# A cross-attention slot reordered: GpSimd's row sums wait for VectorE's next subtraction

## The chip, the cores and the metric

The kernel runs on one core of one Trainium2 chip. The metric is the device time of one execution in microseconds (us). Three runs of the kernel before gave 1718.86, 1724.16 and 1724.18 us; their median is 1724.16 us.

## What is computed

One perceiver layer in fp32: cross attention of 8 batches of 128 queries on 2048 context rows each (width 512, 16 heads of 32), then a causal differential self attention, then a dense mixture of 8 experts. The change touches the cross attention only. Cut to what matters:

```python
q = (layernorm(x) @ wq.T + bq)          # 8 x 128 x 512, heads of 32
k = (ctx @ wk.T + bk)                   # 8 x 2048 x 512
v = (ctx @ wv.T + bv)
scores = einsum('bhqd,bhkd->bhqk', q, k) / sqrt(32)
attn = softmax(scores, axis=-1)
o = einsum('bhqk,bhkd->bhqd', attn, v)  # then x = x + o @ wo.T + bo
...
x = x + differential_attention(layernorm(x)); x = x + experts(layernorm(x))
```

## The kernel before

The cross attention (`cross_attention`) works through 32 score slots (8 batches x 4 head groups; a head group is 4 heads, `HG`). A slot `m` has four chunks `c` = 0 to 3 of 512 context rows, so there are 128 chunks `n = 4m + c`. Beside the scores the same loop projects the keys and values of later context: piece `p` of 512 context rows, in four key products (`keys`) and four value products (`values`), each of 12 matmuls (the fp32 numbers are split into a high and a low half, and `product`, lines 41 to 45, multiplies high with high, high with low and low with high).

Every engine walks the same loop over beats, and a slot is eight beats. In its own walk an engine does, for each beat, what the small functions of lines 475 to 511 name, in the order in which the code asks for them. This order, together with semaphores, is all that sets the order of the work. The text below calls a beat by its remainder r0 to r7 modulo 8.

What a slot does:

- TensorE (lines 757 to 782): at the even beats scores of one chunk into `psS` (`column_scores`, L709: c2 at r0, c3 at r2, c0 at r4, c1 at r6); at every beat one product (r0 to r3 keys, r4 to r7 values); at r2 and r6 the weighted values of two chunks (`outputs`, L723) ahead of the scores; at r0 the denominators (`denominators`, L746), first thing in the beat; at r3 it turns the running maxima (L754, "M"), at r4 the spread maxima back (L754, "B"), after the product of the beat.
- ScalarE (lines 787 to 862): evicts the product of the beat before (L798 keys, L810 and L819 values); at r5 copies the maxima rows (`mb`, L826); at even beats rounds a quarter of the turned context to its high half (L835), at r4 writes `spread` (L838), at even beats takes the exponentials of a chunk (L843), at r0 adds the value bias to the outputs (L850); at odd beats moves a chunk of scores from `psS` to SBUF (L860), which frees `psS` for TensorE.
- VectorE (lines 875 to 923), at even beats: at r4 the maxima per row (`top`, L881); the subtraction of the maxima from a chunk of scores (L888); at r0 reciprocal and division of the outputs (L903, L907); the low half of the context quarter (L911); a transpose of the next quarter (L871); then four maxima over the new scores (L920, L923).
- GpSimd (lines 636 to 651): sums the exponentials of a chunk into `acc`: one addition for c0 (L645, which also waits for the denominators of the slot before), two for the others (L650). It starts when the exponentials of the chunk are done (L640).

The subtraction and the exponentials of chunk n stand ten beats behind its scores: exponentials of c0 at r6, c1 at r0, c2 at r2, c3 at r4. A context quarter has the number k = 0 at r0, 1 at r2, 2 at r4, 3 at r6. The sums of chunk n free a buffer for the move of chunk n + 7 (L859). The outputs of a slot's first chunk wait for the division of the slot before (`od_free`, L718). The last four slots (`TAIL` = 28 on) have no GpSimd sums; TensorE sums their chunks itself (L737), inside `outputs`. No projections are left there from beat 256 on.

Of the kernel before, what the change touches and what calls it, by code (L numbers as in the profile page):

```python
# [47 lines left out]
def f32(ap):  # L48

    return ap.bitcast(F32)  # L50
# [398 lines left out]
def cross_attention(nc, x, ctx_in, w, q_d, o_d, cin, kT, shared):  # L449

    with ExitStack() as ctx:
# [18 lines left out]
        def steps(beat, first, every, count):  # L470

            n, r = divmod(beat - first, every)
            return n if r == 0 and 0 <= n < count else None

        def transposed(beat):

            n = steps(beat, -SLOT, 2, SLOTS * CHUNK)
            return None if n is None or n < 2 * CHUNK else divmod(n, CHUNK)
# [14 lines left out]
        def turned_slot(beat):  # L493
            return steps(beat, 27, SLOT, SLOTS)
# [2 lines left out]
            return steps(beat, 28, SLOT, SLOTS)  # L497

        def exp_step(beat):
            return steps(beat, 30, 2, SLOTS * CHUNK)  # L500

        def value_steps(beat):

# [3 lines left out]
        def sum_slot(beat):  # L507
            return steps(beat, 40, SLOT, SLOTS)

        def normal_slot(beat):  # L510
            return steps(beat, 40, SLOT, SLOTS)


        BANKS = 3
# [119 lines left out]
        @block.gpsimd  # L634
        def _(pool):
            nc.gpsimd.memset(ones[:, :], 1.0).then_inc(const, 1)  # L636
            for n in range(TAIL * CHUNK):
                m, c = divmod(n, CHUNK)
                buf = n % BUFS
                pool.wait_ge(exp_done, n + 1)  # L640
                if c == 0:

                    if m:
                        pool.wait_ge(od_full, m)
                    nc.gpsimd.tensor_tensor(acc[:, :, :], s[:, buf, 0:2, :], s[:, buf, 2:4, :],  # L645
                                            ALU.add).then_inc(sum_done, 1)
                else:
                    for i in range(2):
                        pool.wait_ge(sum_done, m * ADDS + 2 * c - 1 + i)
                        nc.gpsimd.tensor_tensor(acc[:, :, :], acc[:, :, :], s[:, buf, 2 * i:2 * i + 2, :],  # L650
                                                ALU.add).then_inc(sum_done, 1)
# [7 lines left out]
        def _(pe):  # L659
# [97 lines left out]
            for beat in range(FIRST, LAST):  # L757
                for n in value_steps(beat):
                    outputs(n)
                if (m := sum_slot(beat)) is not None and m < TAIL:  # L760
                    denominators(m)
                if (n := score_step(beat)) is not None:
                    column_scores(n)
                if (x0 := projected(beat)) is not None:
                    p, u = x0
                    if u < CHUNK:
                        keys(p, u)
                    else:
                        values(p, u - CHUNK)
                if (m := turned_slot(beat)) is not None:  # L770
                    turn("M", m, mx, mx_done, (m + 1) * MAXIMA)
                if (m := spread_slot(beat)) is not None:
                    turn("B", m, spread, spread_done, m + 1)
                    if m == SLOTS - 1:

                        pe.wait_ge(shared.wo_in, 16)
                        pe.wait_ge(s_moved, SLOTS * CHUNK)
                        for k in range(KD):
                            for o in range(KD):
                                last = nc.tensor.transpose(psS[:, k, o * P:(o + 1) * P],  # L780
                                                           shared.wo[:, o, k * P:(k + 1) * P], ident[:, :])
                            last.then_inc(shared.wo_full, 1)

        @block.scalar
        def _(act):
            act.wait_ge(bias_in, 32)
            for beat in range(FIRST, LAST):
                if beat > FIRST and (x0 := projected(beat - 1)) is not None:
# [32 lines left out]
                if (m := spread_slot(beat - 1)) is not None:  # L821
# [5 lines left out]
                    if m == SLOTS - 1:  # L827
                        for k in range(KD):
                            act.wait_ge(shared.wo_full, k + 1)
                            nc.scalar.activation(shared.woT[0][:, k, :], psS[:, k, :], ACT.Copy).then_inc(shared.wo_hi, 1)  # L830
                if (x0 := transposed(beat)) is not None:
                    p, k = x0

                    act.wait_ge(turned, (p - 2) * CHUNK + k + 1)
                    nc.scalar.activation(cT[0][:, p % 2, k, :], cin[:, 1, k % 2, :], ACT.Copy).then_inc(hi_done, 1)  # L835
                if (m := spread_slot(beat)) is not None:
                    act.wait_ge(top_done, m + 1)
                    nc.scalar.activation(spread[:, :, :], top[:, m % 2, :].rearrange("p (j o) -> p j o", o=1)  # L838
# [1 line left out]
                if (n := exp_step(beat)) is not None:  # L840
                    act.wait_ge(sub_done, n + 1)
                    part = s[:, n % BUFS, :, :].rearrange("p t n -> p (t n)")
                    nc.scalar.activation(part, part, ACT.Exp, scale=SCALE).then_inc(exp_done, 1)  # L843
                if (m := normal_slot(beat)) is not None:
                    g = m % G
                    act.wait_ge(od_free, m + 1)
                    if m >= 2:

                        act.wait_ge(o_out[m % 2], 16 * (m // 2))
                    nc.scalar.activation(o_st[:, m % 2, :], oq[:, :], ACT.Identity,  # L850
                                         bias=bv[:, g:g + 1]).then_inc(o_done, 1)
                if (n := move_step(beat)) is not None:

                    act.wait_ge(mx_done, CHUNK * (n + 1))
                    if n >= BUFS:

                        act.wait_ge(pv_done, n - BUFS + 1)
                        if (n - BUFS) // CHUNK < TAIL:
                            act.wait_ge(sum_done, sums_of(n - BUFS))  # L859
                    nc.scalar.activation(s[:, n % BUFS, :, :].rearrange("p t (j q) -> p t j q", j=HG),  # L860
                                         psS[:, :, :].rearrange("p j (t q) -> p t j q", t=CHUNK),
                                         ACT.Copy).then_inc(s_moved, 1)

        @block.vector
        def _(dve):
            def context_turned(p, k):
# [3 lines left out]
                reached(dve, split_done, u - 2 + 2 * CHUNK + 1 if u >= 2 else 0)  # L870
                nc.vector.transpose(cin[:, 1, k % 2, :], cin[:, 0, k % 2, :]).then_inc(turned, 1)  # L871

            dve.wait_ge(bias_in, 32)
            context_turned(2, 0)
            for beat in range(FIRST, LAST):
                if (m := spread_slot(beat)) is not None:
                    i, bank = RING["M", m, 0], work[BANK["M", m, 0]]
                    dve.wait_ge(work_full, i + 1)

                    reached(dve, spread_done, m - 1)  # L880
                    nc.vector.tensor_reduce(top[:, m % 2, :], bank[:, :].rearrange("p (j k) -> p j k", j=HG),  # L881
                                            AX.X, ALU.max).then_inc(top_done, 1)
                if (n := exp_step(beat)) is not None:
                    m, c = divmod(n, CHUNK)
                    dve.wait_ge(s_moved, n + 1)
                    if c == 0:
                        dve.wait_ge(mb_done, m + 1)
                    nc.vector.tensor_tensor(  # L888
                        s[:, n % BUFS, :, :], s[:, n % BUFS, :, :],
                        mb[:, :].rearrange("p (o n) -> p o n", o=1).broadcast_to([P, CHUNK, HG * P]),  # L890
                        ALU.subtract).then_inc(sub_done, 1)
                if (m := normal_slot(beat)) is not None:
                    if m == SLOTS - 1:
                        for k in range(KD):
                            dve.wait_ge(shared.wo_hi, k + 1)
                            nc.vector.tensor_tensor(shared.woT[1][:, k, :], psS[:, k, :], f32(shared.woT[0][:, k, :]),
                                                    ALU.subtract).then_inc(shared.wo_lo, 1)
                    if m < TAIL:
                        dve.wait_ge(od_full, m + 1)
                    else:  # L900
                        dve.wait_ge(pv_done, (m + 1) * CHUNK)
                    sums = psO[:, P:2 * P] if m < TAIL else work[BANKS - 1][:, 0:P]
                    nc.vector.reciprocal(rD[:, :], sums).then_inc(rd_done, 1)  # L903
                    dve.wait_ge(rd_done, m + 1)

                    reached(dve, o_done, m)
                    nc.vector.tensor_tensor(oq[:, :], psO[:, 0:P], rD[:, :], ALU.mult).then_inc(od_free, 1)  # L907
                if (x0 := transposed(beat)) is not None:
                    p, k = x0
                    dve.wait_ge(hi_done, p * CHUNK + k + 1)  # L910
                    nc.vector.tensor_tensor(cT[1][:, p % 2, k, :], cin[:, 1, k % 2, :], f32(cT[0][:, p % 2, k, :]),  # L911
                                            ALU.subtract).then_inc(split_done, 1)
                if (x0 := turned_next(beat)) is not None:
                    context_turned(*x0)
                if (n := score_step(beat)) is not None:
# [1049 lines left out]
```

## Time and profile before

| | |
|---|---|
| profiled execution, own time | 1722.41 us |
| its span, first to last instruction | 1720.6 us |
| mean granted TensorE clock | 0.978 |
| TensorE matmul busy | 1618.0 us (94%) |
| VectorE busy | 1264.2 us (73%) |
| ScalarE busy | 941.5 us (55%) |
| GpSimd busy | 676.6 us (39%) |

The cross attention's steady part lies between about 180 and 1057 us of the span. In the rows PE is TensorE's matmul, PEld its weight load, DVE is VectorE, ACT ScalarE, POOL GpSimd. A row of the timeline gives start, duration (both us), engine, line, what is written and read, the number of merged instructions, and in brackets how long the engine had been idle and what ended the wait. Consecutive instructions of VectorE and ScalarE overlap by some 0.1 us, so the distance from one start to the next is a little shorter than the duration.

### The profile page before, as it was taken

The page shows a single profiled execution, that of the slowest core. Times are in us where ns is not written, and L with a number is a line of the kernel's source. Part 1 is how long each engine was busy: PE and PEld are TensorE (multiplying, and loading weights), DVE is VectorE, ACT ScalarE, POOL GpSimd, SP SyncE. Part 2 cuts the span into 40 slices and gives each one's busy share as a digit, 9 for nine tenths or more (in the row PEclk, how much of TensorE's full clock was granted, in tenths as well). Part 3 has the DMA queues.
Part 4 walks back from the last instruction along what each step waited for, and adds up shares of the span by engine and source line. Part 5 has one row for each costly group of instructions (what it writes and reads, how often), then busy time and mean ns, then how long its engine had stood idle before and what let it go on. Part 6 is the DMA issues. An engine that isn't in the chain of part 4 may idle for free. (4 is left out here: it accounts for less than half of the span.)

```text
span 1720.6 us, 36999 instructions
## 1 busy us (share of the span) xinstructions
PE 1618.0 (94%) x15604; PEld 1310.2 (76%) x15604; DVE 1264.2 (73%) x1643; ACT 941.5 (55%) x1437; POOL 676.6 (39%) x352
## 2 busy tenths in 40 slices
PE   7999999999999999999999999768899799999999
PEld 6777777777777777777777777657787677777787
DVE  5248998999899899989998997877633577753322
ACT  4347666766666766666666666653201777631000
POOL 0004565655556555556555566102000244432210
PEclk9999999999999999999999999879899899899999
DMA  5322222222222222222222220213323111211001
GB/s 183 75 43 39 35 37 37 35 35 40 38 37 37 37 35 35 37 36 36 36 41 34 37 37 7 77 48 114 135 86 99 62 50 50 64 50 49 25 25 50
DMA packets 310404, 88.75 MB, mean 52 GB/s; under 512 B 259392, under 2 KB 292160, under 8 KB 310240
## 3 DMA queue, kind: packets, MB, share of 16 engines
q1 hardware_dynamic: 310240, 86.39, 21.7%
q8 instruction: 124, 2.03, 0.5%
q14 instruction: 40, 0.33, 0.1%
HBM read 71.67 MB, written 14.68 MB: 50 GB/s over the span
## 5 line engine op out<-in xcount | busy, mean ns | idle before, releaser
L650 POOL TENSOR_TENSOR b_acc<-b_acc,b_s 128x1024 f32<-128x1024 f32 x168 | 462.5, 2753 | 250.6 <-ACT b_s L843 243.6
L923 DVE TENSOR_TENSOR b_mx<-b_psS,b_mx 128x512 f32<-128x512 f32 x480 | 328.1, 684 | 26.4 <-PE b_psS L709 13.3
L888 DVE TENSOR_TENSOR b_s<-b_s,b_mb 128x2048 f32<-128x2048 f32 x128 | 340.8, 2664 | 3.2 <-ACT b_mb L826 3.2
L860 ACT ACTIVATE b_s<-b_psS 128x2048 f32<-128x2048 f32 x128 | 241.0, 1883 | 150.4 <-DVE b_mx L923 150.4
L843 ACT ACTIVATE b_s<-b_s 128x2048 f32<-128x2048 f32 x128 | 245.3, 1916 | 68.4 <-DVE b_s L888 68.4
L43 PE MATMUL b_work<-wvT,cT 128*128 128x512 f32 x496 | 203.0, 409 | 0.0
L43 PE MATMUL b_work<-cT,wkT 128*128 128x512 f32 x496 | 200.3, 404 | 1.7 <-POOL b_ones L636 1.7
L709 PE MATMUL b_psS<-b_q,b_kT 32*128 32x128 f32 x4096 | 153.9, 287 | 47.6 <-ACT b_s L860 47.5
L44 PE MATMUL b_work<-wvT,cT 128*128 128x512 f32 x496 | 194.5, 392 | 0.0
L44 PE MATMUL b_work<-cT,wkT 128*128 128x512 f32 x496 | 194.2, 392 | 0.0
L45 PE MATMUL b_work<-wvT,cT 128*128 128x512 f32 x496 | 193.8, 391 | 0.0
L45 PE MATMUL b_work<-cT,wkT 128*128 128x512 f32 x496 | 193.7, 390 | 0.0
L911 DVE TENSOR_TENSOR cT<-cin,cT 128x512 fp32r<-128x512 f32 x120 | 158.1, 1317 | 41.0 <-ACT cT L835 40.9
L709 PEld LDWEIGHTS b_psS<-b_q,b_kT 32*128 32x128 f32 x4096 | 130.1, 190 | 74.5 <-issue 74.5
L645 POOL TENSOR_TENSOR b_acc<-b_s 128x1024 f32<-128x1024 f32 x28 | 94.5, 3375 | 207.0 <-PE b_psO L746 133.4
L723 PE MATMUL b_psO<-b_s,v_sb 128*32 128x128 f32 x4096 | 130.3, 279 | 2.5 <-issue 1.8
L798 ACT ACTIVATE b_kT<-b_work,b_bk 128x512 f32<-128x512 f32 x124 | 84.9, 685 | 86.1 <-PE b_work L45 86.1
L723 PEld LDWEIGHTS b_psO<-b_s,v_sb 128*32 128x32 f32 x4096 | 110.9, 112 | 25.1 <-issue 24.6
L43 PEld LDWEIGHTS b_work<-cT,wkT 128*128 128x128 f32 x496 | 93.0, 187 | 27.4 <-POOL b_ones L636 2.1
L43 PEld LDWEIGHTS b_work<-wvT,cT 128*128 128x128 f32 x496 | 93.1, 188 | 24.6
L45 PEld LDWEIGHTS b_work<-wvT,cT 128*128 128x128 f32 x496 | 93.2, 188 | 20.6
L45 PEld LDWEIGHTS b_work<-cT,wkT 128*128 128x128 f32 x496 | 93.1, 188 | 20.5
(290 smaller groups left out, 2780.8 us busy)
## 6 DMA issues: line engine op xcount, KB each, us to landing
cin<-in_ctx SPq DMA_DIRECT2D x480, 64.0 KB, 2.3
experts_sb<-in_L_ffn_expert_w SPq DMA_DIRECT2D x8, 1024.0 KB, 5.4
q_scratch<-d_st SPq DMA_DIRECT2D x16, 256.0 KB, 2.3
k_scratch<-d_st SPq DMA_DIRECT2D x16, 256.0 KB, 2.3
e_q<-q_scratch SPq DMA_DIRECT2D x16, 256.0 KB, 2.7
k_sb<-k_scratch SPq DMA_DIRECT2D x16, 256.0 KB, 2.9
cin<-in_ctx SPq DMA_DIRECT2D x4, 512.0 KB, 8.5
b_kT<-in_x SPq DMA_DIRECT2D x4, 512.0 KB, 8.1
```

Of the source, the lines that this page charges most:

```text
L43: nc.tensor.matmul(out, lhs[0], rhs[0], start=first, stop=False)
L44: nc.tensor.matmul(out, lhs[0], rhs[1], start=False, stop=False)
L45: return nc.tensor.matmul(out, lhs[1], rhs[0], start=False, stop=last)
L645: nc.gpsimd.tensor_tensor(acc[:, :, :], s[:, buf, 0:2, :], s[:, buf, 2:4, :], ALU.add).then_inc(sum_done, 1)
L650: nc.gpsimd.tensor_tensor(acc[:, :, :], acc[:, :, :], s[:, buf, 2 * i:2 * i + 2, :], ALU.add).then_inc(sum_done, 1)
L709: last = nc.tensor.matmul(psS[:, j, t * P:(t + 1) * P], kT[h, at + t * P:at + (t + 1) * P], q[h, m % 3, :], start=True, stop=True)
L723: last = nc.tensor.matmul(psO[j * HD:(j + 1) * HD, 0:P], v[:, at + j * HD:at + (j + 1) * HD], s[:, n % BUFS, i, j * P:(j + 1) * P], start= ...
L843: nc.scalar.activation(part, part, ACT.Exp, scale=SCALE).then_inc(exp_done, 1)
L860: nc.scalar.activation(s[:, n % BUFS, :, :].rearrange("p t (j q) -> p t j q", j=HG), psS[:, :, :].rearrange("p j (t q) -> p t j q", t=CHUN ...
L888: nc.vector.tensor_tensor(s[:, n % BUFS, :, :], s[:, n % BUFS, :, :], mb[:, :].rearrange("p (o n) -> p o n", o=1).broadcast_to([P, CHUNK, ...
L911: nc.vector.tensor_tensor(cT[1][:, p % 2, k, :], cin[:, 1, k % 2, :], f32(cT[0][:, p % 2, k, :]), ALU.subtract).then_inc(split_done, 1)
L923: nc.vector.tensor_tensor(mx[:, :, :], part, mx[:, :, :], ALU.max).then_inc(mx_done, 1)
```

## The change

Four things are altered in `cross_attention`; the arithmetic is the same.

1. GpSimd's sums of chunk n wait, beside the exponentials of n, for the subtraction of chunk n + 1 and for the low half that VectorE does in that same beat.
2. VectorE's order in an even beat becomes: low half (odd k), subtraction, low half (even k), `top`, division, transpose, maxima. Before it was `top`, subtraction, division, low half, transpose, maxima.
3. ScalarE rounds the high half for an odd k at the end of the beat before (after the move), for an even k where it did; the output bias comes after the move.
4. TensorE does the denominators after the beat's scores and product instead of ahead of them, and the division and the bias of slots below 28 stand at r1 (beat 41) instead of r0 (beat 40). SyncE's store of the output follows one beat later for those slots.

```diff
         def exp_step(beat):
-            return steps(beat, 30, 2, SLOTS * CHUNK)
+            return steps(beat, exp_beat(0), 2, SLOTS * CHUNK)
+
+        def exp_beat(n):
+            return 30 + 2 * n
...
+        def late_slot(beat):
+            m = steps(beat, 40, SLOT, SLOTS)
+            return m if m is not None and m >= TAIL else None
+
         def normal_slot(beat):
-            return steps(beat, 40, SLOT, SLOTS)
+
+            m = steps(beat, 41, SLOT, TAIL)
+            return late_slot(beat) if m is None else m
...
                 pool.wait_ge(exp_done, n + 1)
+
+                pool.wait_ge(sub_done, n + 2)
+                x0 = transposed(exp_beat(n + 1))
+                if x0 is not None:
+                    p, k = x0
+                    pool.wait_ge(split_done, p * CHUNK + k + 1)
...
                 for n in value_steps(beat):
                     outputs(n)
-                if (m := sum_slot(beat)) is not None and m < TAIL:
-                    denominators(m)
                 if (n := score_step(beat)) is not None:
                     column_scores(n)
...
+                if (m := sum_slot(beat)) is not None and m < TAIL:
+                    denominators(m)
                 if (m := turned_slot(beat)) is not None:
                     turn("M", m, mx, mx_done, (m + 1) * MAXIMA)
...
+            def context_hi(p, k):
+                act.wait_ge(turned, (p - 2) * CHUNK + k + 1)
+                nc.scalar.activation(cT[0][:, p % 2, k, :], cin[:, 1, k % 2, :], ACT.Copy).then_inc(hi_done, 1)
...
-                if (x0 := transposed(beat)) is not None:
-                    p, k = x0
-
-                    act.wait_ge(turned, (p - 2) * CHUNK + k + 1)
-                    nc.scalar.activation(cT[0][:, p % 2, k, :], cin[:, 1, k % 2, :], ACT.Copy).then_inc(hi_done, 1)
+                x0 = transposed(beat)
+                if x0 is not None and not x0[1]:
+
+                    context_hi(*x0)
...
-                if (m := normal_slot(beat)) is not None:
-                    g = m % G
-                    act.wait_ge(od_free, m + 1)
...
+                if (m := normal_slot(beat)) is not None:
+                    g = m % G
+                    act.wait_ge(od_free, m + 1)
...
+                x0 = transposed(beat + 1)
+                if x0 is not None and x0[1]:
+                    context_hi(*x0)
...
+            def context_lo(p, k):
+                dve.wait_ge(hi_done, p * CHUNK + k + 1)
+                nc.vector.tensor_tensor(cT[1][:, p % 2, k, :], cin[:, 1, k % 2, :], f32(cT[0][:, p % 2, k, :]),
+                                        ALU.subtract).then_inc(split_done, 1)
...
             for beat in range(FIRST, LAST):
-                if (m := spread_slot(beat)) is not None:
-                    i, bank = RING["M", m, 0], work[BANK["M", m, 0]]
-                    dve.wait_ge(work_full, i + 1)
...
+                x0 = transposed(beat)
+                if x0 is not None and x0[1]:
+                    context_lo(*x0)
                 if (n := exp_step(beat)) is not None:
                     m, c = divmod(n, CHUNK)
                     dve.wait_ge(s_moved, n + 1)
...
                         ALU.subtract).then_inc(sub_done, 1)
+                if x0 is not None and not x0[1]:
+                    context_lo(*x0)
+                if (m := spread_slot(beat)) is not None:
+                    i, bank = RING["M", m, 0], work[BANK["M", m, 0]]
+                    dve.wait_ge(work_full, i + 1)
...
-                if (x0 := transposed(beat)) is not None:
-                    p, k = x0
-                    dve.wait_ge(hi_done, p * CHUNK + k + 1)
-                    nc.vector.tensor_tensor(cT[1][:, p % 2, k, :], cin[:, 1, k % 2, :], f32(cT[0][:, p % 2, k, :]),
-                                            ALU.subtract).then_inc(split_done, 1)
```

## Rows read from the trace of the kernel before

**Rows 1.** Windows of 100 us: length, busy per engine (instructions), granted clock, DMA share, GB/s.

```profile
600.00:700.00 100.00, 96.28 (x1124) 77.94 (x1123) 91.69 (x93) 67.96 (x69) 58.35 (x21) 1.00 0.21 36
1100.00:1200.00 100.00, 73.02 (x1262) 63.14 (x1263) 76.23 (x98) 54.50 (x51) 10.54 (x12) 0.79 0.25 81
```

**Rows 2.** Timeline of TensorE in one slot.

```profile
617.34 0.65 PE L746 MATMUL b_psO<-b_acc,b_ones 128*32 128x128 f32 x16
619.23 1.17 PE L709 MATMUL b_psS<-b_q,b_kT 32*128 32x128 f32 x32 [1.24 <-ACT b_s L860]
...
626.00 1.96 PE L723 MATMUL b_psO<-b_s,v_sb 128*32 128x128 f32 x64
```

**Rows 3.** Timeline of VectorE over the same slot, and the top of a late one.

```profile
601.51 0.69 DVE L881 TENSOR_REDUCE b_top<-b_work 128x4 f32<-128x512 f32 x1 [2.22 <-PE b_work L754]
602.12 2.28 DVE L888 TENSOR_TENSOR b_s<-b_s,b_mb 128x2048 f32<-128x2048 f32 x1
604.32 0.69 DVE L911 TENSOR_TENSOR cT<-cin,cT 128x512 fp32r<-128x512 f32 x1
604.92 0.71 DVE L871 STREAM_TRANSPOSE cin<-cin 128x512 f32<-128x512 f32 x1
...
608.29 2.69 DVE L888 TENSOR_TENSOR b_s<-b_s,b_mb 128x2048 f32<-128x2048 f32 x1
611.33 2.47 DVE L911 TENSOR_TENSOR cT<-cin,cT 128x512 fp32r<-128x512 f32 x1 [0.35 <-ACT cT L835]
...
614.35 2.82 DVE L923 TENSOR_TENSOR b_mx<-b_psS,b_mx 128x512 f32<-128x512 f32 x4
...
619.29 0.95 DVE L903 RECIPROCAL b_rD<-b_psO 128x128 f32<-128x128 f32 x1
620.27 0.29 DVE L907 TENSOR_TENSOR b_oq<-b_psO,b_rD 128x128 f32<-128x128 f32 x1
...
625.47 3.59 DVE L888 TENSOR_TENSOR b_s<-b_s,b_mb 128x2048 f32<-128x2048 f32 x1
...
635.25 0.69 DVE L881 TENSOR_REDUCE b_top<-b_work 128x4 f32<-128x512 f32 x1 [2.22 <-PE b_work L754]
```

**Rows 4.** Timeline of GpSimd over the same slot.

```profile
606.43 6.82 POOL L650 TENSOR_TENSOR b_acc<-b_acc,b_s 128x1024 f32<-128x1024 f32 x2 [4.23 <-ACT b_s L843]
618.16 3.46 POOL L645 TENSOR_TENSOR b_acc<-b_s 128x1024 f32<-128x1024 f32 x1 [4.92 <-PE b_psO L746]
621.97 4.93 POOL L650 TENSOR_TENSOR b_acc<-b_acc,b_s 128x1024 f32<-128x1024 f32 x2 [0.35 <-ACT b_s L843]
631.08 4.86 POOL L650 TENSOR_TENSOR b_acc<-b_acc,b_s 128x1024 f32<-128x1024 f32 x2 [4.18 <-ACT b_s L843]
```

**Rows 5.** Timeline of ScalarE over the same slot.

```profile
610.66 0.63 ACT L835 ACTIVATE cT<-cin 128x512 fp32r<-128x512 f32 x1
...
617.21 1.88 ACT L860 ACTIVATE b_s<-b_psS 128x2048 f32<-128x2048 f32 x1 [1.88 <-DVE b_mx L923]
618.98 0.59 ACT L819 ACTIVATE v_sb<-b_work 128x512 f32<-128x512 f32 x1
```

**Rows 6.** Timeline of the first slots: a ScalarE move and a TensorE score row.

```profile
137.38 1.90 ACT L860 ACTIVATE b_s<-b_psS 128x2048 f32<-128x2048 f32 x1
...
180.62 1.17 PE L709 MATMUL b_psS<-b_q,b_kT 32*128 32x128 f32 x32 [0.66 <-ACT b_s L860]
```

**Rows 7.** Timeline of TensorE where the projections end (beats 256 to 258).

```profile
1089.09 0.64 PE L746 MATMUL b_psO<-b_acc,b_ones 128*32 128x128 f32 x16
1089.66 1.17 PE L709 MATMUL b_psS<-b_q,b_kT 32*128 32x128 f32 x32
1091.18 1.08 PE L723 MATMUL b_psO<-b_s,v_sb 128*32 128x128 f32 x32 [0.35 <-issue]
...
1093.80 1.08 PE L737 MATMUL b_work<-b_s,b_ones 128*32 128x128 f32 x32
1095.92 1.17 PE L709 MATMUL b_psS<-b_q,b_kT 32*128 32x128 f32 x32 [1.03 <-ACT b_s L860]
```

## What the change is predicted to do

> **What bounds the kernel now.** I read the windows of 100 us first. In the steady cross attention TensorE is busy 96.3 of 100 us and VectorE 91.7 [rows 1]: TensorE is nearly full, and VectorE is close enough to hold it up. So the timeline of one slot comes next, engine by engine. A slot lasts 635.25 - 601.51 = 33.74 us [rows 3], and TensorE waits once in it: its scores of r0 stand 1.24 us idle until ScalarE's move has emptied psS [rows 2]. The denominators start at 617.34 and these scores at 619.23; where nothing is waited for, the same pair is 1089.66 - 1089.09 = 0.57 us apart [rows 2, 7]. So the stall costs 1.89 - 0.57 = 1.32 us, and TensorE's own work is 32.4 us per slot. That is the floor of any reordering here: 1.3 us x 26 slots = 34 us, 2%.
>
> Why the move is late is read backwards. The move starts at 617.21 [rows 5], when VectorE's maxima end at 614.35 + 2.82 = 617.17; these began late because the low half before them took 2.47 us instead of 0.69, and the subtraction before that 2.69 instead of 2.28 [rows 3]. Beside them runs GpSimd's pair of additions from 606.43, 6.82 us instead of 4.86 [rows 4]. The stretched cases show a strict turn-taking: GpSimd's pair ends at 621.97 + 4.93 = 626.90, and the subtraction that VectorE started at 625.47 ends at 629.06, 2.16 us later, its whole undisturbed length [rows 3, 4]. It made no headway while the addition ran. The transpose at 604.92 and the maxima keep their length everywhere.
>
> The Trainium skill, page "SBUF — State Buffer", section "Who interferes with whom", says that a VectorE instruction with two SBUF inputs and a GpSimd instruction that reads SBUF exclude each other for the whole instruction, whichever came first running on. If bandwidth were split instead, the collisions below would cost about half and the first rival would be right; by the page's rule and by the row above they cost in full.
>
> **What the change removes.** Per slot VectorE is stretched by 0.41 (608.29) + 1.78 (611.33) + 1.31 us (625.47) [rows 3], and by about 1.0 more at the low half of r0, which I read off no row here and don't need below. It also waits 2.22 us for TensorE at `top` [rows 3]. The new order fills that wait with a subtraction, and GpSimd no longer starts just ahead of a subtraction or low half. What is late next decides, so I walk one slot of the new order from rows.
>
> **The new loop.** Units: a subtraction 2.28 us, next start after 2.20; a low half 0.60 to the next start; `top` 0.61; a transpose and four maxima 3.37 to the next start, 0.08 more to their end (604.92 to 608.29) [rows 3]; two additions 4.87 [rows 4]; a move 1.77 to the next start, a high half 0.63 [rows 5]. One engine reacts to another after 0.04 us (617.17 to 617.21) [rows 3, 5]. Time zero is the end of the subtraction of c0 at r6.
> - GpSimd may now start the sums of c3: 0.1 to 5.0. It has two waits more per chunk than before; no row prices them, so from nothing to the 0.17 us between denominators and sum (617.99 to 618.16) [rows 2, 4]; I take 0.05 to 0.1.
> - VectorE does transpose and maxima, to 3.4, and at once wants the subtraction of c1. The second addition still runs. The subtraction ends 2.16 after it: 7.1, not 5.6.
> - Low half, transpose, maxima of r0: to 11.1.
> - ScalarE moves, adds the bias (0.3) and only then makes the high half k = 1: to 13.8. VectorE, done with the division (0.98 + 0.29 from 11.0) [rows 3], waits 1.6 us for it.
> - Low half, subtraction of c2: to 16.7. GpSimd sums c1 from 16.8 to 21.7.
> - Transpose and maxima to 20.1; the subtraction of c3 runs into the second addition again and ends at 23.8, not 22.3.
> - Low half, `top`, transpose, maxima: to 28.4.
> - Move, high half k = 3: to 30.9; VectorE has waited 2.5 us. Low half, subtraction of c0: 33.8.
>
> So the loop closes at 33.8 us without TensorE in it, where the loop of before, through TensorE, closed at 33.74. VectorE loses 1.5 + 1.5 us to GpSimd instead of 4.5, and 4.1 us to ScalarE's late high halves instead of 2.6. TensorE's scores of r0 start after the move of c1, at 3.4 + 1.9 + 0.1 = 5.4, and TensorE idles 33.8 - 32.4 = 1.4 us per slot: some 1.1 there and 0.3 at r4, where the move of c3 ends at 22.0.
>
> **Edits taken at nothing.** The denominators wait for the sums of c3 (5.0) and come at about 9.5: covered by 4 us. The division needs them at 11.0; they end near 10.1. GpSimd's one addition of c0 waits for them too: 10.3 to 12.7 (two thirds of the 3.46 us row [rows 4], which had a subtraction in its way), clear of the low half at 13.85 by 1.1. The outputs of r2 come two products after r0's scores (626.00 - 619.23 = 6.77 [rows 2], plus 0.57 for the denominators): 12.7, against the division's 12.3. The later sums free a buffer for the move seven chunks on, which comes at least 7 us after them. SyncE's store waits for the bias at 13.3; behind it in its queue stands the next context load, whose transpose comes only at 16.7.
>
> **The edges.** First slots: `top` now stands behind the low half, the first maxima end 0.6 later, the move at 137.38 goes to 137.9, the high half k = 3 to 140.3, the subtraction of c0 to 143.2. One loop without its first collision and bias, 33.0, gives 176.2, and the scores of r0 come at 181.6 instead of 180.62 [rows 6]: +1.0 us. End: at beat 258 TensorE's outputs stand ahead of its scores and wait for the division, which now follows the maxima of beat 256. Before, outputs ran at 1091.18. Now: scores at 1089.66, ready at 1090.9, maxima to 1093.7, division to 1094.9, outputs with their sums 3.7 us (1091.18 to 1094.88), next scores 1098.7 instead of 1095.92 [rows 7]: +2.8. In these last slots the granted clock falls (0.79 over the window) [rows 1], so `top` behind the subtraction gives nothing back before the very last slot, some 0.3. Together +2.5.
>
> **The sum.** 26 x (33.8 - 33.74) = +1.6, edges +1.0 and +2.5: +5.1 us on the profiled execution's 1722.4 (span 1720.6 and 1.8 around it): 1727.5. The median of the runs shown lies 1.8 above the profiled one; I give 1728. My reading of waits carries some 0.15 us per slot, 4 us in all.
>
> **Rivals.**
> *The stretches simply go.* If a blocked subtraction loses nothing, the walk gives maxima of r6 ending at 30.7 in a frame where TensorE needs its scores at 32.4: the move ends at 32.65, a stall of 0.4, slots of 32.8. 26 x -0.95 = -25, with the edges -21: 1701. For it: the stretches of before are gone at three of four places. Against: VectorE reaches the subtraction 3.3 us after GpSimd may start, and two additions take 4.9. Chance 0.18.
> *ScalarE's queue at r4 and r5 joins the loop (slower).* After `top` it must do spread, exponentials, an eviction and the `mb` copy (0.57 + 1.8 + 0.5 + 0.5) before the move of c0; VectorE's transpose and maxima take 3.4 over the same time. The margin is 0.1 us; beyond it each delay adds in full. Evictions behind a late product are the place; at 0.5 us per slot: +13, 1741. Chance 0.12.
> *A third collision (slower).* If the denominators end 1.1 us later than I have them, the sum of c0 meets the low half k = 1, for 0 to 2.3 us; at half of that 26 x 1.2 = +31: 1758. Chance 0.08.
> The forecast keeps 0.62.
>
> **How the numbers follow.** About 0.3% (5.2 us) is what a measurement can tell from no change. The forecast's +5 sits on that bound: of its 0.62, 0.31 within, 0.26 slower, 0.05 faster. With the rivals: faster 0.23, same 0.31, slower 0.46. The likeliest case alone spans 1722 to 1734. The range leaves out half of the first rival and the third collision: 1704 to 1743.
>
> **What the profile would show.** Right: slots of 33.7 to 33.9 us; subtractions of 3.7 us or so twice a slot (c1, c3) and of 2.28 else; all low halves at 0.69; VectorE waiting for the high half 1.6 and 2.5 us; no wait at `top`; 4.9 us for every pair of additions; outputs at beat 258 waiting for the division. Wrong: a slot near 32.8, or a low half above 0.69, or ScalarE's move of c0 not starting right behind the maxima.

## The result and the profile after

The changed kernel takes 1757.45 us (median of 4 runs, 1755.87 to 1765.41), the kernel before 1723.07 us: a ratio of 1.0213, 95% interval 1.0178 to 1.0249. It is slower by 2.1%, where 1728 was forecast with a range of 1704 to 1743. The profiled execution has a span of 1754.1 us, 33.5 more than before.

One correction comes first, since everything hangs on it. The text of the change above says "odd k" and "even k" for the context quarters. The code says `x0[1]` and `not x0[1]`, which is k > 0 and k = 0. So ScalarE's early high half, and VectorE's low half ahead of the subtraction, hold for k = 1, 2 and 3, also for k = 2 at r4. I read the condition wrongly and walked the wrong order.

Windows of 100 us of the changed kernel (length, busy per engine, granted clock, DMA share, GB/s), beside [rows 1]:

```profile
600.00:700.00 100.00, 94.45 (x1110) 74.82 (x1109) 79.31 (x88) 66.23 (x67) 46.99 (x20) 1.00 0.21 35
1100.00:1200.00 100.00, 71.94 (x1328) 62.29 (x1330) 75.59 (x77) 61.94 (x50) 12.95 (x6) 0.83 0.18 54
```

TensorE, VectorE and GpSimd are all busy for a smaller share of the window, in a slot that is 1.1 us longer: everybody waits more. The waits from 200 to 1000 us (total us, times, longest) say for what:

```profile
DVE cT L896 <- ACT cT L803: 149.2, 69, 2.5
ACT b_spread L856 <- DVE b_top L921: 68.6, 23, 3.0
PE b_psS L724 <- ACT b_s L870: 29.5, 24, 1.3
PE b_work L769 <- ACT b_spread L856: 13.2, 23, 0.6
```

VectorE waits for ScalarE's high half three times a slot, 6.5 us in all. TensorE's stall at r0 is what it was (1.3 us), and it has a new one of 0.6 at the turn of r4. VectorE over one slot, which lasts 634.35 - 599.51 = 34.84 us, to be held against [rows 3]:

```profile
599.51 3.87 DVE L910 TENSOR_TENSOR b_s<-b_s,b_mb 128x2048 f32<-128x2048 f32 x1
603.30 0.68 DVE L896 TENSOR_TENSOR cT<-cin,cT 128x512 fp32r<-128x512 f32 x1
...
610.11 0.69 DVE L896 TENSOR_TENSOR cT<-cin,cT 128x512 fp32r<-128x512 f32 x1 [1.56 <-ACT cT L803]
610.71 2.28 DVE L910 TENSOR_TENSOR b_s<-b_s,b_mb 128x2048 f32<-128x2048 f32 x1
612.92 0.70 DVE L892 STREAM_TRANSPOSE cin<-cin 128x512 f32<-128x512 f32 x1
613.54 2.83 DVE L949 TENSOR_TENSOR b_mx<-b_psS,b_mx 128x512 f32<-128x512 f32 x4
618.83 0.69 DVE L896 TENSOR_TENSOR cT<-cin,cT 128x512 fp32r<-128x512 f32 x1 [2.46 <-ACT cT L803]
619.44 2.28 DVE L910 TENSOR_TENSOR b_s<-b_s,b_mb 128x2048 f32<-128x2048 f32 x1
621.65 0.68 DVE L921 TENSOR_REDUCE b_top<-b_work 128x4 f32<-128x512 f32 x1
...
628.16 0.69 DVE L896 TENSOR_TENSOR cT<-cin,cT 128x512 fp32r<-128x512 f32 x1 [2.46 <-ACT cT L803]
628.77 2.28 DVE L910 TENSOR_TENSOR b_s<-b_s,b_mb 128x2048 f32<-128x2048 f32 x1
...
634.35 3.88 DVE L910 TENSOR_TENSOR b_s<-b_s,b_mb 128x2048 f32<-128x2048 f32 x1
```

All low halves are at 0.69 us and only one subtraction a slot is long, so the turns lost to GpSimd fell from 4.5 to 1.6 us per slot: what the change does at the port works. The wait in front of 618.83 is the piece that the prediction did not have. The same stretch on ScalarE:

```profile
616.40 1.89 ACT L870 ACTIVATE b_s<-b_psS 128x2048 f32<-128x2048 f32 x1 [0.35 <-DVE b_mx L949]
618.19 0.61 ACT L803 ACTIVATE cT<-cin 128x512 fp32r<-128x512 f32 x1
...
622.36 0.63 ACT L856 ACTIVATE b_spread<-b_top 128x512 f32<-128x512 f32 x1 [2.98 <-DVE b_top L921]
...
625.18 0.59 ACT L845 ACTIVATE b_mb<-b_work 128x512 f32<-128x512 f32 x1
625.73 1.88 ACT L870 ACTIVATE b_s<-b_psS 128x2048 f32<-128x2048 f32 x1
```

The move (616.40) starts as soon as VectorE's maxima end, then comes the high half, then the low half: maxima, move, high half, low half, with VectorE idle for the middle two.

And GpSimd:

```profile
606.57 2.42 POOL L660 TENSOR_TENSOR b_acc<-b_s 128x1024 f32<-128x1024 f32 x1 [5.34 <-PE b_psO L761]
613.13 4.91 POOL L665 TENSOR_TENSOR b_acc<-b_acc,b_s 128x1024 f32<-128x1024 f32 x2 [4.15 <-DVE b_s L910]
621.86 4.88 POOL L665 TENSOR_TENSOR b_acc<-b_acc,b_s 128x1024 f32<-128x1024 f32 x2 [3.82 <-DVE b_s L910]
631.19 4.89 POOL L665 TENSOR_TENSOR b_acc<-b_acc,b_s 128x1024 f32<-128x1024 f32 x2 [4.45 <-DVE b_s L910]
```

Every pair now takes its own 4.9 us, against 6.82 in one place before [rows 4]. The pair from 631.19 ends at 636.08, and the subtraction started at 634.35 ends at 638.23, 2.15 later: the one turn still lost.

### The profile page after: what moved, and what is told of

Its sections match the earlier page's. It is cut to its first block and busy times, and to the rows that moved or that the text cites. A ratio compares the mean times of both kernels' runs of the same rounds, so it can differ in the third digit from the quotient of the medians.

```text
span 1754.1 us, 37092 instructions
## 1 busy us (share of the span) xinstructions
PE 1630.6 (93%) x15589; PEld 1306.6 (74%) x15604; DVE 1187.7 (68%) x1643; ACT 942.8 (54%) x1437; POOL 591.6 (34%) x352
## 5 line engine op out<-in xcount | busy, mean ns | idle before, releaser
L665 POOL TENSOR_TENSOR b_acc<-b_acc,b_s 128x1024 f32<-128x1024 f32 x168 | 404.1, 2405 | 354.0 <-DVE b_s L910 347.5
L896 DVE TENSOR_TENSOR cT<-cin,cT 128x512 fp32r<-128x512 f32 x120 | 82.7, 689 | 211.1 <-ACT cT L803 211.1
L660 POOL TENSOR_TENSOR b_acc<-b_s 128x1024 f32<-128x1024 f32 x28 | 67.6, 2414 | 221.4 <-PE b_psO L761 142.7
L43 PEld LDWEIGHTS b_work<-cT,wkT 128*128 128x128 f32 x496 | 93.2, 188 | 32.7 <-issue 5.6
L1727 ACT ACTIVATE e_sm<-e_psS,e_low 128x128 f32<-128x128 f32 x256 | 90.1, 383 | 34.6 <-DVE e_low L1802 34.6
```

The lines of the kernel that those rows point to most:

```text
L43: nc.tensor.matmul(out, lhs[0], rhs[0], start=first, stop=False)
L1727: last = nc.scalar.activation(sm[:, hf, i, j % 2, u, :], psS[:, j, u, :], ACT.Exp, bias=low[:, hf, j, u:u + 1], scale=-1.0, accum_out=sums ...
```

## The experiments

The slot is taken between the first and the last row of the maxima per row in about 225 to 1012 us (19 to 25 of them), divided by their distance in slots. The ratio is to the kernel before on the same chip. In e5 and e9 "tiny sums" means that GpSimd adds only 8 of the 512 columns; they leave out most of the denominators and serve to price the additions.

| kernel | median us | ratio (95%) | slot us |
|---|---|---|---|
| before | 1723 | | 33.74 |
| changed | 1757.45 | 1.0213 (1.0178 to 1.0249) | 34.86 |
| e1 odd k only | 1731.96 | 1.0056 (1.0039 to 1.0072) | 33.94 |
| e2 high half before the move | 1702.81 | 0.9877 (0.9859 to 0.9896) | 32.76 |
| e3 changed, no new GpSimd waits | 1923.64 | 1.1172 (1.1153 to 1.1190) | 40.94 |
| e4 before + GpSimd waits | 1711.13 | 0.9932 (0.9916 to 0.9949) | 33.20 |
| e5 changed, tiny sums | 1745.32 | 1.0147 (1.0117 to 1.0177) | 34.37 |
| e6 e2 + division back at r0 | 1694.86 | 0.9836 (0.9819 to 0.9852) | 32.50 |
| e7 e4 + row maxima late | 1686.44 | 0.9807 (0.9778 to 0.9837) | 32.42 |
| e8 e2, no new GpSimd waits | 1870.66 | 1.0830 (1.0755 to 1.0906) | 39.16 |
| e9 e8, tiny sums | 1700.87 | 0.9888 (0.9853 to 0.9922) | 32.76 |
| e10 before + row maxima late | 1767.63 | 1.0245 (1.0215 to 1.0275) | 35.20 |

**e1, the order that the prediction walked.**

```diff
-                if x0 is not None and x0[1]:
+                if x0 is not None and x0[1] % 2:
...
-                if x0 is not None and not x0[1]:
+                if x0 is not None and not x0[1] % 2:
```

(on ScalarE and on VectorE alike)

> The changed kernel with one condition altered: the early high half and the early low half for odd k only (k = 1 and 3), so that k = 2 at r4 has its high half in the beat and its low half behind the subtraction. Theory (the walk of the prediction is right, it only read the condition as odd where it says k > 0): the loop closes at 33.8 us instead of 34.84, two long subtractions of about 3.8 us per slot (c1, c3), VectorE waits 1.6 and 2.5 us for the high half, in all 1757 - 26 x 1.0 = 1730 us. Rival (the cost lies in GpSimd's waits or in the moved denominators, which stay): the slot stays near 34.8 us and the time within 5 us of 1757.

Measured: 1731.96 us, slot 33.94. VectorE:

```profile
604.52 3.89 DVE L910 TENSOR_TENSOR b_s<-b_s,b_mb 128x2048 f32<-128x2048 f32 x1
608.34 0.68 DVE L896 TENSOR_TENSOR cT<-cin,cT 128x512 fp32r<-128x512 f32 x1
...
621.64 3.87 DVE L910 TENSOR_TENSOR b_s<-b_s,b_mb 128x2048 f32<-128x2048 f32 x1
```

These are the two long subtractions, c3 (604.52) and c1 (621.64), that the prediction's walk had, and k = 2 follows c3 at once. One condition carries 1757.45 - 1731.96 = 25.5 of the 34 us. The other 9 us are what the walked order itself costs against the kernel before, where the forecast had 5. e1 alters the condition on both engines, so it does not tell ScalarE's part from VectorE's; e2 does for ScalarE's.

**e2, the high half before the move.**

```diff
+                x0 = transposed(beat + 1)
+                if x0 is not None and x0[1]:
+                    context_hi(*x0)
                 if (n := move_step(beat)) is not None:
...
-                x0 = transposed(beat + 1)
-                if x0 is not None and x0[1]:
-                    context_hi(*x0)
```

> The changed kernel with ScalarE's high half for k > 0 put before the move of its odd beat instead of after it. Theory (the loop over maxima, move, high half, low half sets the slot): VectorE's 6.5 us of waits for the high half go, the loop falls to about 31 us, TensorE's own 32.4 us become the bound with at most a few tenths of stall, and the time is 1757 - 26 x 2.3 = about 1697 us; low halves of k = 1 and 2 then run into GpSimd's additions (up to 2 us long). Rival (GpSimd's additions against VectorE set the slot whatever ScalarE does): the waits for the high half turn into blocked low halves and the slot stays above 33.7 us, the time above 1724.

Measured: 1702.81 us, slot 32.76: faster than both kernels. TensorE's records leave no gap in the window, and a low half meets GpSimd for 0.7 us at k = 1 (610.70), beside 0.1 us at k = 3:

```profile
600.00:700.00 100.00, 100.00 (x1138) 80.04 (x1137) 85.46 (x97) 69.17 (x70) 52.27 (x22) 1.00 0.23 38
```

```profile
605.53 0.69 DVE L896 TENSOR_TENSOR cT<-cin,cT 128x512 fp32r<-128x512 f32 x1 [1.24 <-ACT cT L803]
...
610.70 1.43 DVE L896 TENSOR_TENSOR cT<-cin,cT 128x512 fp32r<-128x512 f32 x1
```

The three instructions were there before; only their place behind a move of 1.9 us made them part of the loop. The remaining 6 us to the expected 1697 are the slot: 34.84 - 2.3 = 32.54 was expected, and the 0.22 us above it are 6 us in 26 slots. TensorE shows no gap, so these are its own work, and the kernel before has less of it. The denominators (L761) now stand between two products:

```profile
604.28 1.17 PE L724 MATMUL b_psS<-b_q,b_kT 32*128 32x128 f32 x32
...
608.32 0.65 PE L761 MATMUL b_psO<-b_acc,b_ones 128*32 128x128 f32 x16
...
611.88 1.95 PE L738 MATMUL b_psO<-b_s,v_sb 128*32 128x128 f32 x64
```

From these scores to the outputs it is 7.60 us; before, it was 6.77, and 0.57 for the denominators in front of the scores [rows 2, 7]. The move of the denominators, which the prediction took at nothing, costs TensorE 0.26 us per slot.

**e3, the changed kernel without GpSimd's waits** (the six lines after `pool.wait_ge(exp_done, n + 1)` out).

> The changed kernel without GpSimd's two new waits (its sums start with the exponentials, as before), everything else as changed. Theory (order of the high halves sets the slot, GpSimd's waits are worth 1 to 2 us): the long subtraction of c1 moves to another place, the sums of c3 and c1 meet low halves and subtractions, and the slot is 34.8 to 36 us: 1757 to 1785 us. Rival (GpSimd's waits are what cost): back to 33.7 us per slot, about 1727 us.

Measured: 1923.64 us, slot 40.94. Both expectations miss by far. The direction of the theory held, its size did not. The worst place is r2, right behind VectorE's wait for ScalarE:

```profile
605.88 2.65 DVE L890 TENSOR_TENSOR cT<-cin,cT 128x512 fp32r<-128x512 f32 x1 [1.56 <-ACT cT L797]
608.45 4.48 DVE L904 TENSOR_TENSOR b_s<-b_s,b_mb 128x2048 f32<-128x2048 f32 x1
```

Lost turns need not be all of it: the mean granted clock from 200 to 1000 us is 0.91 here and 1.00 in the changed kernel. No run tells how much of the slot that is.

**e4, GpSimd's waits alone, on the kernel before** (the same six lines in).

> The kernel before with GpSimd's two new waits alone; no order of VectorE, ScalarE or TensorE is altered. Theory (walk over rows): the low half of r6 is no longer blocked, TensorE's stall at r0 falls from 1.3 to about 0.3 us plus some 0.3 us of waiting for the later sums at the denominators, a slot takes about 33.0 us: 1723 - 26 x 0.7 = 1705 us. Rival (GpSimd's waits cost, since its sums come later): the denominators wait for the sums ahead of the scores and the slot is 34 us or more, 1730 us and up.

Measured: 1711.13 us, slot 33.20: the waits by themselves win 0.7%, 12 of the 18 us that were expected. TensorE's stall for the move at r0, 29.8 us in the kernel before from 200 to 1000 us, is gone from the list of waits. In its place is the price that was foreseen, TensorE's denominators behind the later sums, with 15.4 us, 0.6 per slot where 0.3 was expected:

```profile
PE b_psO L752 <- POOL b_acc L656: 15.4, 24, 0.9
```

**e5, the price of the one turn still lost** (in `acc` and `s` of both additions `0:8` for the last index; `acc` is set to 1.0 once at the start).

> The changed kernel with every GpSimd addition cut to 8 of the 512 columns (all waits stay; the denominators are therefore not those of the softmax, which this kernel leaves out). It prices the one lost turn that is left, the subtraction of c1. Theory (loop of maxima, move, high half, low half): the long subtraction of 3.87 us becomes 2.28, but the low half k = 0 then waits for its own high half, so only about 0.7 of the 1.6 us come off: slot 34.1 us, 1757 - 18 = 1739 us. Rival (the lock between GpSimd and VectorE is what made the changed kernel slow): slot at or below the 33.7 us of before, 1724 us or less.

Measured: 1745.32 us, slot 34.37, 0.5 us less. Of the 1.6 us of the long subtraction two thirds turn into waits for high halves, 0.75 us at k = 0 and 0.25 more at k = 2:

```profile
630.42 2.28 DVE L911 TENSOR_TENSOR b_s<-b_s,b_mb 128x2048 f32<-128x2048 f32 x1
633.45 0.69 DVE L897 TENSOR_TENSOR cT<-cin,cT 128x512 fp32r<-128x512 f32 x1 [0.75 <-ACT cT L804]
```

So with almost nothing left of GpSimd's work the new order is still slower than the kernel before. The slowdown is ScalarE's order, not the port.

**e6, denominators, division and bias back at r0, on e2** (`denominators` ahead of `column_scores`; `normal_slot` as before; the division behind the subtraction, the bias behind the exponentials).

> e2 (high half before the move) with denominators, division and bias back at r0 where they stood before the change. Theory: the steady slot stays at 32.7 us (the division fits into VectorE's 1.2 us wait for the high half k = 0), and the 3 to 4 us that the moved division costs where the projections end come back: 1703 - 3.5 - 1 = 1698 us. Rival (the moved denominators are what lets TensorE run free): scores of r0 wait for the sums again, slot 33.2 us or more, 1712 us and up.

Measured: 1694.86 us, slot 32.50, where 32.7 was expected: with the denominators beside the scores the 0.26 us that e2 found in TensorE's own work come back. Between the profiled executions of e2 and e6 that is 7.1 us in 27 slots, of which the start takes 2.9 back (the first of these scores of r0 at 178.38 in e2, 181.31 in e6). The other 4.4 are at the end. From TensorE's scores of beat 256 to the first product of the output projection it is 90.3 us (1058.73 to 1149.0) against 94.7 in e2 (1062.91 to 1157.6): the moved division costs 4.4 us at the end, where the walk had 2.8. In e2 TensorE stands in front of these outputs:

```profile
1068.31 1.94 PE L738 MATMUL b_psO<-b_s,v_sb 128*32 128x128 f32 x32 [3.65 <-issue]
```

TensorE idles 3.65 us ahead of these outputs, which wait for the division as walked, and then runs in part at the lower of its two clock levels (1.2 GHz; granted clock 0.50 from 1068 to 1070): 1.94 us for what takes 1.06 to 1.08 at the higher. Outputs with their sums take 1073.22 - 1068.31 = 4.9 us where the walk had 3.7, which is most of the rest.

**e7, the row maxima behind subtraction and low half, on e4.** VectorE's block of `spread_slot` (L876 to L882 of before) moves ahead of `turned_next`.

> e4 (the kernel before with GpSimd's new waits alone) with one order of VectorE altered: the row maxima of r4 behind subtraction and low half. Theory: VectorE's wait of 2.28 us for TensorE at the row maxima is filled, its loop shortens by 0.6 us, the slot falls from 33.18 to 32.6 us: 1711 - 15 = 1696 us. Rival (the subtraction of r4 then meets GpSimd's second addition and loses what it gained): slot unchanged at 33.1 us, 1709 to 1713 us.

Measured: 1686.44 us, slot 32.42, which is TensorE's own work as worked out from [rows 2] and [rows 7]. It is the fastest kernel of the study, 1.9% below the kernel before (0.7% came from the waits alone). Its VectorE still loses 3.7 us per slot to GpSimd, on subtractions only:

```profile
600.00:700.00 100.00, 100.00 (x1181) 80.85 (x1180) 93.27 (x97) 71.05 (x73) 50.52 (x21) 1.00 0.22 37
```

```profile
613.56 3.75 DVE L887 TENSOR_TENSOR b_s<-b_s,b_mb 128x2048 f32<-128x2048 f32 x1
617.70 0.69 DVE L910 TENSOR_TENSOR cT<-cin,cT 128x512 fp32r<-128x512 f32 x1 [0.39 <-ACT cT L841]
...
622.53 3.15 DVE L887 TENSOR_TENSOR b_s<-b_s,b_mb 128x2048 f32<-128x2048 f32 x1 [0.17 <-ACT b_mb L832]
```

**e8, e2 without GpSimd's waits.**

> e2 (high half before the move) without GpSimd's two new waits. Theory (in e3 GpSimd took the port just while VectorE stood waiting for its high half, so that both operations behind that wait lost a turn; with the high half early there is no such gap): far better than e3's 1924 us, near the kernel before, 1715 to 1735 us, some 20 us above e2. Rival (without the waits any of the new orders loses a turn at nearly every operation): 1800 us and more.

Measured: 1870.66 us, slot 39.16. My explanation of e3, that GpSimd took the port while VectorE stood waiting for a high half, fell: those waits are mostly gone here and the kernel is nearly as slow. VectorE and GpSimd, both of e8:

```profile
622.89 2.42 POOL L654 TENSOR_TENSOR b_acc<-b_s 128x1024 f32<-128x1024 f32 x1 [14.04 <-PE b_psO L755]
625.46 12.37 POOL L659 TENSOR_TENSOR b_acc<-b_acc,b_s 128x1024 f32<-128x1024 f32 x4
```

```profile
623.99 1.87 DVE L890 TENSOR_TENSOR cT<-cin,cT 128x512 fp32r<-128x512 f32 x1
625.78 4.46 DVE L904 TENSOR_TENSOR b_s<-b_s,b_mb 128x2048 f32<-128x2048 f32 x1
...
633.53 2.07 DVE L890 TENSOR_TENSOR cT<-cin,cT 128x512 fp32r<-128x512 f32 x1
635.52 4.45 DVE L904 TENSOR_TENSOR b_s<-b_s,b_mb 128x2048 f32<-128x2048 f32 x1
```

A low half and the subtraction right behind it each stand behind an addition: while the low half runs, the next addition is already queued and goes first when it ends. Three subtractions of 4.45 us and three stretched low halves make some 10 us per slot. GpSimd is held up in turn: its four additions take 12.37 us instead of 4 x 2.42 = 9.7, and the 2.7 more are one subtraction and one low half. Two of the three places are these four additions without a pause, behind GpSimd's 14 us wait for the denominators; the third is the pair that sums c3 (603.68, 5.18 us). In no row of the waits from 200 to 1000 us does another engine wait for GpSimd's sums. The mean granted clock over that stretch is 0.96.

**e9, e8 with tiny sums.**

> e8 (high half before the move, no new GpSimd waits, 1871 us) with every GpSimd addition cut to 8 of 512 columns; the denominators are therefore not those of the softmax. Theory (the 10 us of stretched operations per slot seen in e8 are lost turns at the shared port and carry all of its loss): the stretches go, TensorE's 32.4 us are the bound, 1695 to 1705 us. Rival (the sums' late chain through the denominators or the order itself costs): above 1750 us.

Measured: 1700.87 us, slot 32.76, the same slot as e2. With the additions short, all 6.4 us of e8's loss per slot are gone, so it is neither the order nor the wait for the denominators (16.2 us here). Short additions also shorten GpSimd's chain; that the chain as such did not hold anybody up is read from e8's waits, where nobody waits for the sums. The lost turns are what is left, with the lower clock: from 200 to 1000 us its mean is 1.00 in e9.

**e10, the row maxima late, alone, on the kernel before.**

> The kernel before with one order of VectorE altered: the row maxima of r4 behind subtraction and low half; GpSimd has no new wait. Together with e4 (waits alone, 33.18 us per slot) and e7 (both, 32.42) it completes the square. Theory (both parts shorten the same loop: filling the 2.2 us wait at the row maxima is worth more than TensorE's 1.3 us stall by itself): slot 32.5 to 33.0 us, 1690 to 1705 us. Rival (without the waits the subtraction brought forward meets GpSimd's additions and each operation of VectorE loses a turn, as in e3 and e8): slot above 33.7 us, slower than the kernel before.

Measured: 1767.63 us, slot 35.20. The rival was right. The same reordering that is worth 1.3% on top of GpSimd's waits (e4 to e7) costs 2.5% without them:

```profile
619.24 2.68 DVE L881 TENSOR_TENSOR b_s<-b_s,b_mb 128x2048 f32<-128x2048 f32 x1
622.36 2.36 DVE L904 TENSOR_TENSOR cT<-cin,cT 128x512 fp32r<-128x512 f32 x1 [0.44 <-ACT cT L835]
...
628.87 3.55 DVE L881 TENSOR_TENSOR b_s<-b_s,b_mb 128x2048 f32<-128x2048 f32 x1 [0.17 <-ACT b_mb L826]
632.34 2.90 DVE L904 TENSOR_TENSOR cT<-cin,cT 128x512 fp32r<-128x512 f32 x1
```

In the kernel before, the 2.22 us of waiting at the row maxima [rows 3] were also a gap in which GpSimd ran a pair at its own length (631.08, 4.86 us [rows 4]). Filled with a subtraction, the gap is gone: the low half of r4 goes from 0.69 to 2.36 us and that of r6 from 2.47 to 2.90. Some 6 us of the time, 0.4%, are the granted clock in later stages (last section).

## Why the prediction was wrong, point by point

- **What bounds the kernel.** Right for the order of before: TensorE's own work is 32.4 us per slot, and e7 has a slot of 32.42 and no gap. Wrong as "the floor of any reordering here": with the denominators between two products it is 32.76 (e2 and e9, neither with a gap). The walk moved them at their old 0.57 us; from scores to outputs of r2 the changed kernel takes 7.63 us instead of 7.34. It did not decide the result, since TensorE waits here in any case.
- **The turn-taking at the port.** Right, in kind and size: 3.87 to 3.89 us for a subtraction behind an addition (3.8 walked). e8 and e9 show what turns can cost: 10 us of stretched instructions, 6.4 us of slot.
- **The new loop: the step that failed.** The walk gave k = 2 its high half in the beat and its low half behind the subtraction of c3. The code has both the other way round. With the end of the subtraction of c0 as zero (596.21 in the rows of after), the walk and the chip agree up to there: the subtraction of c1 ends at 7.1 walked and 7.2 measured, that of c2 at 16.7 and 16.8. Then the walk has 23.8 for c3 and the chip 25.5 (619.44 + 2.28), since VectorE waits 2.46 us for the high half where the walk had a lost turn of 1.5; after it 28.4 and 29.5, and 33.8 and 34.8 for the loop. That 1.0 us in 26 slots is 26 us, nearly all of the 28.4 by which the 33.5 measured on the span exceed the 5.1 forecast. e1, which has the order that was walked, closes at 33.94 and takes 1732 us.
- **The edges.** The first stalled scores of r0 come at 183.29 (181.6 walked), and from those of beat 248 to the output projection it is 1215.26 - 1088.94 = 126.3 us against 1180.85 - 1057.22 = 123.6 before, +2.7 (+2.5 walked). The start is the same quarter again: the first loop takes 35.1 us (142.73 to 177.86) where the walk writes 33.0 without its terms, and e1's takes 32.9. The terms of the 33.5 us of span are then +2.7 at the start, 905.65 - 876.60 = +29.05 in 26 slots, +2.7 at the end, and -0.9 in the later stages. In e1 they are +1.7, +5.1 and +3.9: the walk's 1.0, 1.6 and 2.5 were all too small, at a third to two thirds of it. GpSimd's start behind a subtraction measured 0.14 us (631.05 to 631.19), where 0.05 to 0.1 was taken. The forecast's own sum for the profiled execution, 1727.5, with the 1.8 us to the median that it names, gives 1729.3 and not 1728.
- **TensorE's stalls.** At r0 1.1 us was forecast and 1.28 to 1.29 measured (1.10 in e1). At r4 0.3 was forecast, for the scores behind the move of c3. Neither kernel has that one: in e1 TensorE waits at r0 only, and the 0.3 is its own work at the denominators. The changed kernel waits 0.6 at the turn of r4 instead, since the row maxima stand behind one more wait.
- **The rivals.** None of the three is what happened. The stretches did go, for the most part, but the loop through ScalarE took their place. ScalarE's queue at r5 ends level with VectorE's maxima (the move at 625.73, the maxima at 625.70), as the forecast had it, and decides nothing. The third collision, whose 1758 is close to the time measured, did not occur: the low half at 610.11 takes 0.69 us, 1.1 us after GpSimd's addition ended. The nearness of the number is chance.
- **What the rivals should have held.** A wait of VectorE for ScalarE stood in the forecast's own list twice, at 4.1 us per slot, more than all turns lost. That it would be more if a third quarter joined was one reading of a condition away.

## What to carry to other kernels

A step moved "earlier" in an engine's own order is earlier only if it passes what waits: behind a move that itself waits for VectorE, the high half was late for the very engine it was to serve, and one place further up it was worth 3% (e2 against the changed kernel). Two orders that each look like a gain can depend on each other: e10 loses 2.5% alone and wins 1.3% on top of e4, because the idle time that it fills was the other engine's turn. Read a condition by what it is true for, value by value, before walking a schedule with it.

## What the runs showed that was not expected

Two engines that exclude each other instruction by instruction can lock into alternation. With a chain of additions waiting, each low half and subtraction of VectorE stands behind a full addition, and a kernel that needs 32.8 us per slot with tiny sums (e9) takes 39.2 with whole ones (e8). The Trainium skill, page "SBUF — State Buffer", section "Who interferes with whom", says that issue order decides who blocks. The trace agrees: in e8 the subtraction that starts 0.3 us after an addition (625.78 behind 625.46) takes 4.46 us.

The granted clock fell for a stretch in the self attention in some executions, at a place that no experiment touched. Windows of 50 us from 200 us after the first product of the output projection, e6 and then e7:

```profile
1349.00:1399.00 50.00, 49.51 (x367) 39.14 (x372) 34.93 (x90) 36.11 (x160) 21.22 (x37) 0.93 0.14 43
```

```profile
1344.00:1394.00 50.00, 49.73 (x391) 39.65 (x390) 38.78 (x101) 37.48 (x172) 22.05 (x39) 1.00 0.17 54
```

From that first product to the end, e2, e6, e8 and e10 take 545.8 to 546.0 us, e1, e3, e5, e7, e9 and the changed kernel 538.8 to 538.9, the kernel before and e4 539.7. One kernel can have both: the four runs of e2 are 1699.71 and 1700.31 us with a mean granted clock of 0.978 and 0.977, and twice 1705.32 with 0.973; those of e7 are 1684.70 to 1686.83 (0.977 to 0.978) and 1696.09 (0.971). So 7 of the 12 us between the profiled executions of e6 and e7 are this. All four runs of e6 have the lower clock (0.972 to 0.973), so that the order of the work has a part in it is not excluded. Why it falls in one execution and not in another stays open.
